# Ternary gate and up weights kept in SBUF, and the first codes and gate product made in the second attention's end

## The chip, the cores and the metric

The kernel runs on one core of one Trainium2 chip. The metric is the device time of one execution in microseconds (us). A core has five engines that run their own instruction streams and meet in semaphores: TensorE (PE, matmuls, with its weight loads shown as PEld), VectorE (DVE), ScalarE (ACT), GpSimd (POOL) and SyncE (SP, which here issues the DMAs). SBUF is the working memory of 128 partitions, PSUM holds the eight banks that TensorE writes.

## The reference, cut to what matters

Four layers of attention and feed-forward run over `x` (2, 256, 512), that is four tiles of 128 rows. The change lies in layer 1: its attention (16 heads with low-rank projections), and its feed-forward, for which the reference computes in this manner:

```python
def int4_quant(x):
    beta = jnp.mean(jnp.abs(x), axis=-1, keepdims=True)
    x_q = jnp.clip(jnp.round(x * SQRT7 / (beta + EPS)), -8, 7)
    return x_q * (beta * SQRT7) / SQRT7
def bitlinear(x, w, scale):
    w_mean = jnp.mean(jnp.abs(w))
    w_q = jnp.clip(jnp.round(w / (w_mean + EPS)), -1.0, 1.0)
    return jnp.einsum('...i,oi->...o', x, w_q * w_mean * scale)
```

The normalised rows are quantised to four bits (the "codes"). Gate and up products with ternary weights (1376 x 512) follow, then relu squared of the gate times the up product, an eight-bit quantisation of that (by its row maximum), and the down product (512 x 1376), which is added to `x`. All three weights must be summed over their absolute values before one of them can be rounded.

## The kernel before, in words

Each layer part is a function with one block, in which every engine has its own program; all engines meet in a barrier between blocks. The order on each engine is written out by hand. Three stages matter: `layer1_attention` (from 73 us to 184 us of the span), `layer1_ffn` (184 to 233 us) and then `layer2_attention`.

**`layer1_attention`** runs 64 steps `u`, one for a head of one of the four row tiles (16 steps a tile, so tile t is done after step 16t + 15). In a step PE makes the scores of step u + 3, turns the exponentials of step u (L976) and mixes; DVE takes the row maximum (`maximum`, L1070); ACT makes the exponentials (L1174) and copies three turned tiles of four out of PSUM (L1183), DVE the fourth (`copy_turned`, L1094). Into these steps DVE has other work woven: at steps 40, 45, 50 and 55 the counts of a bisection that belongs to a later layer (L2394), at steps 53 and 54 the division and addition for the tile before (L1080, L1087), then the row statistics (L1131 to L1137), and at steps 59, 60 and 62 the normalised rows of tiles 0, 1 and 2 (`tile_rows_vector`, L267). These need `rstd`, which POOL makes with one power instruction each (L274). After step 63 the last tile goes through ACT's `copy_mixed` (L1190), PE's `turn_mixed` (L1006), `divide_mixed` and `add_mixed`, and the block ends.

**The ternary weights.** During these steps POOL rounds the weights (`ternary_round_gpsimd`, L400, L402 and L404, three instructions a piece) in 13 pieces: four of gate and four of up (128 x 1376), three of down (128 x 1536) and two small ones of down. SP loads a piece into one of two buffers, and stores the rounded piece to HBM (`ternary_round_sync`, L419). POOL's three `rstd` instructions stand behind all thirteen pieces. The first instructions of `layer1_ffn` on SP read all of it back, six DMAs for gate and up (L1263) and two for down.

**`layer1_ffn`** begins with the statistics of tile 3 on DVE (L257 to L261) while ACT sums the magnitudes of all four tiles (L1288). `quantise4` (L1328) makes the codes of two tiles at a time on DVE: three small instructions, scaling (L1339), rounding (L1342), clipping (L1345), and three small ones for the scales. PE turns the codes (L1422), ACT copies them, and the gate and up products follow in three chunks of columns (512, 512, 352; `gate_up`, L1440). Of each chunk ACT makes relu and square (L1309, L1314), and DVE the product with up (`inner_chunk`, L1363). PE may fill a bank pair again when ACT and DVE have read the chunk two before. For each tile DVE then finds the maximum (`magnitude`, L1368), scales (L1378) and rounds (L1383); PE turns the result (`turn8`, L1435) and makes the down product (`down`, L1464). DVE has two bisection counts ahead of the first chunks (L1390 to L1394). PE's last work in the stage is woven with key and value products for the next layer (`first_group_kv`, L1541), whose weights POOL splits when they are loaded (L1522 to L1531).

## Time and profile before

| what | value |
|---|---|
| median of 3 runs | 852.37 us (851.94 to 855.39) |
| profiled execution, its own time | 853.51 us |
| its span | 851.8 us |
| busy in the span | PE 773.4, PEld 628.2, DVE 692.9, ACT 517.0, POOL 433.0 us |
| mean granted TensorE clock | 0.978 of full speed |
| HBM read and written | 60.28 MB and 5.34 MB |

The span is what the profiler shows from the first to the last instruction; the execution's own time lies 1.7 us above it. PE is busy for 91% of the span, DVE for 81%. Such shares say little of a stage that takes 49 us of 852: in the windows from 184.3 to 233.2 us PE is busy for 38.98 us and DVE for 39.77 us of 48.90, and the granted clock is 0.90. What a change in this stage is worth is read from the timeline there. A timeline row gives start, duration, engine, line and operation, and in brackets how long the engine had been idle before it and what it waited for; a row with xN merges N instructions.

### The profile page before, as it was taken

Reading aid. Unit: us, or ns where it says so; the run is one execution under the profiler, and the core shown is the slowest. Engines: PE = TensorE matmul, PEld = TensorE weight load, DVE = VectorE, ACT = ScalarE, POOL = GpSimd, SP = SyncE. Lnnn points to the kernel's source line nnn. Section 1 sums busy time; section 2 is a strip of 40 time slices with the busy share of each in tenths; the row PEclk is TensorE's granted clock in tenths of the full one; section 3 lists DMA queues with packets and bytes.
Section 4 is the critical chain, followed back from the end, with each engine's and each line's share of the span. In section 5 each row is a group of like instructions: output and inputs, shape, how many; then the busy total and the mean of one; then the engine's idle time right before and its main releaser. Section 6 shows DMA issues by size and latency. Waiting matters only on the chain. (4 is left out here: it accounts for less than half of the span.)

```text
span 851.8 us, 16376 instructions
## 1 busy us (share of the span) xinstructions
PE 773.4 (91%) x5134; PEld 628.2 (74%) x5140; DVE 692.9 (81%) x1766; ACT 517.0 (61%) x1401; POOL 433.0 (51%) x388
## 2 busy tenths in 40 slices
PE   1976799948988999999999999999999999988888
PEld 0474566634677898888888888989888889776447
DVE  7878998969787887887887788788878878876986
ACT  6875789846457657657657656665675675641421
POOL 3236068825134755745746746745754764665110
PEclk9999999978999999999999999999999999999999
DMA  8244136535030320320220320220310210003001
GB/s 308 99 167 157 64 116 218 187 119 181 0 100 1 100 76 1 99 74 0 99 74 0 99 74 0 99 61 13 99 49 25 74 50 25 26 1 118 3 0 50
DMA packets 37773, 66.15 MB, mean 78 GB/s; under 512 B 5537, under 2 KB 17889, under 8 KB 37602
## 3 DMA queue, kind: packets, MB, share of 16 engines
q1 hardware_dynamic: 37730, 65.63, 23.4%
q8 instruction: 21, 0.34, 0.2%
q14 instruction: 22, 0.18, 0.1%
HBM read 60.28 MB, written 5.34 MB: 77 GB/s over the span
## 5 line engine op out<-in xcount | busy, mean ns | idle before, releaser
L2394 DVE TENSOR_SCALAR_CACHE_REDUCE xn<-ctxT,candidate 128x512 bf16<-128x512 f32 x240 | 168.8, 741 | 0.0
L2041 ACT ACTIVATE layer_attention_probs<-xnT,stats 128x512 f32<-128x512 f32 x128 | 93.9, 734 | 114.6 <-DVE stats L2176 114.6
L2188 DVE TENSOR_TENSOR layer_attention_probsT<-bank,layer_attention_probsT 128x512 fp32r<-128x512 f32 x128 | 88.1, 688 | 50.5 <-ACT layer_attention_probsT L2049 49.3
L1780 PE MATMUL bank<-layer_attention_keysT,layer_attention_queriesT 128*128 128x512 f32 x384 | 121.8, 425 | 5.0 <-DVE layer_attention_queriesT L2169 5.0
L1780 PEld LDWEIGHTS bank<-layer_attention_probsT,layer_attention_values 128*128 128x128 f32 x768 | 99.1, 189 | 13.5 <-DVE layer_attention_probsT L2188 5.2
L2049 ACT CAST layer_attention_probsT<-bank 128x512 fp32r<-128x512 f32 x128 | 74.9, 585 | 52.7 <-PE bank L1857 52.6
L1780 PE MATMUL bank<-layer_attention_probsT,layer_attention_values 128*128 128x256 f32 x768 | 102.3, 282 | 4.1 <-DVE layer_attention_probsT L2188 3.0
L1780 PE MATMUL bank<-layer_attention_l_wq,layer_attention_xnT 128*128 128x512 f32 x408 | 99.3, 392 | 0.1
L1780 PEld LDWEIGHTS bank<-layer_attention_l_wkv,layer_context_parts 128*128 128x128 f32 x720 | 88.3, 188 | 2.8
L1780 PE MATMUL bank<-layer_attention_l_wkv,layer_context_parts 128*128 128x256 f32 x720 | 90.3, 278 | 0.0
L1780 PE MATMUL bank<-layer_attention_wo,layer_attention_headsT 128*128 128x512 f32 x336 | 88.8, 406 | 0.0
L2176 DVE CUSTOM_DVE_ANT_0 xnT<-bank,layer_attention_mask 128x512 f32<-128x512 f32 x128 | 87.1, 680 | 0.6 <-PE bank L1780 0.5
L1780 PEld LDWEIGHTS bank<-layer_attention_l_wq,layer_attention_xnT 128*128 128x128 f32 x408 | 75.3, 188 | 16.0 <-issue 0.2
L1723 POOL TENSOR_TENSOR layer_attention_mixed<-layer_attention_mixed,xnT 128x512 f32<-128x512 f32 x30 | 49.0, 1633 | 70.1 <-DMA xnT<-inverse_sums 49.5
L1857 PE MATMUL bank<-ident,layer_attention_probs 128*128 128x128 f32 x512 | 76.9, 273 | 3.0 <-ACT layer_attention_probs L2041 3.0
L1857 PEld LDWEIGHTS bank<-ident,layer_attention_probs 128*128 128x128 f32 x512 | 61.2, 140 | 14.2 <-issue 4.0
L1780 PEld LDWEIGHTS bank<-layer_attention_keysT,layer_attention_queriesT 128*128 128x128 f32 x384 | 63.0, 191 | 11.6 <-issue 5.8
L1780 PEld LDWEIGHTS bank<-layer_attention_wo,layer_attention_headsT 128*128 128x128 f32 x336 | 60.0, 189 | 11.5
L1708 POOL TENSOR_SCALAR layer_attention_ssq<-layer_attention_ssq 128x4 f32<-128x4 f32 x48 | 9.7, 202 | 87.5 <-ACT layer_attention_squares L2000 87.5
L2000 ACT ACTIVATE layer_attention_squares<-bank 128x128 f32<-128x128 f32 x192 | 52.0, 298 | 0.0
L1174 ACT ACTIVATE layer_attention_probs<-bank,layer_attention_negmax 128x512 f32<-128x512 f32 x64 | 44.9, 706 | 11.0 <-DVE layer_attention_negmax L1070 10.7
L1710 POOL TENSOR_TENSOR layer_attention_ssq<-layer_attention_ssq,minus_half 128x4 f32<-128x4 f32 x48 | 48.8, 1018 | 4.0
(340 smaller groups left out, 1645.5 us busy)
## 6 DMA issues: line engine op xcount, KB each, us to landing
layer_attention_l_raw_qo<-in_wqT SPq DMA_DIRECT2D x8, 1024.0 KB, 5.5
layer_attention_l_raw_qo<-in_woT SPq DMA_DIRECT2D x8, 1024.0 KB, 6.6
xnT<-inverse_sums SPq DMA_DIRECT2D x15, 512.0 KB, 3.7
tw_raw<-in_w_gateT SPq DMA_DIRECT2D x8, 688.0 KB, 5.5
tw_raw<-in_w_upT SPq DMA_DIRECT2D x8, 688.0 KB, 4.2
tw_raw<-in_w_downT SPq DMA_DIRECT2D x6, 768.0 KB, 4.6
layer_attention_l_raw_kv<-in_wkvT SPq DMA_DIRECT2D x8, 512.0 KB, 4.8
ternary<-tw_rounded SPq DMA_DIRECT2D x8, 344.0 KB, 2.5
```

The lines of the kernel that those rows point to most:

```text
L1174: a.activation(probs[:, u % 4, :], S[u % 3][:, :], ACT.Exp, bias=negmax[:, tile(u), head(u):head(u) + 1], accum_out=sums[:, tile(u), head( ...
L1708: own(g.tensor_scalar(ssq[:, c, :], ssq[:, c, :], 1.0 / HD, EPS, ALU.mult, ALU.add))
L1710: own(g.tensor_tensor(ssq[:, c, :], ssq[:, c, :], k.minus_half[:, 0:REP], ALU.pow))
L1723: g.tensor_tensor(now, now, factors, ALU.mult).then_inc(S_["mix_scaled"], 1)
L1780: last = pe.matmul(out, stationary[f][a], moving[f][b], start=f == 0 and x == 0, stop=f == count - 1 and x == 2)
L1857: last = pe.transpose(T[u % 2][:, c * P:(c + 1) * P], probs[:, u % 3, c * P:(c + 1) * P], k.ident[:, :])
L2000: return a.activation(squares[:, h, :], source, ACT.Square, accum_out=ssq[:, c, h:h + 1])
L2041: a.activation(probs[:, u % 3, :], masked[:, u % 2, :], ACT.Exp, bias=negmax[:, u:u + 1], scale=-1.0, accum_out=sums[:, u:u + 1]).then_inc ...
L2049: a.copy(probsT[:, 0, p % 2, :, u % 2 * P:(u % 2 + 1) * P], T[u % 2][:, :].rearrange("p (c q) -> p c q", c=CPB)).then_inc(S_["probsT_high" ...
L2176: v.tensor_tensor_reduce(masked[:, u % 2, :], S[u % 2][:, :], mask[:, u % TPB, :], -1.0, 3.4e38, ALU.add, ALU.min, negmax[:, u:u + 1]).the ...
L2188: v.tensor_tensor(probsT[:, 1, p % 2, :, columns], T[u % 2][:, :].rearrange("p (c q) -> p c q", c=CPB), probsT[:, 0, p % 2, :, columns], A ...
L2394: own(k.nc.vector.tensor_scalar((k.flags if flags is None else flags)[:, r % 2], row_tile(k.ctxT, r), k.candidate[:, r:r + 1].bitcast(F32) ...
```

## The change

**Memory.** A new `Region` on the other side of SBUF holds what was allocated apart: the query weights of the attention (`raw_qk`, `wqk`), and over them, once they are spent, the rounded gate and up weights (`gate_up`), then in layer 2 `wo`, `mask` and `mixed`. POOL writes rounded gate and up pieces straight into `gate_up`; only down pieces are still stored to HBM and read back. The pieces come in another order: down first, then gate, then up. From the third gate piece on they overlay `wqk`, so POOL first waits for the last query product (`BESIDE_WQK`).

**`rstd`.** POOL makes it for tile 0 after 6 pieces, for tile 1 after 10, for tile 2 after all 13. DVE makes the rows of tiles 0, 1 and 2 at steps 52, 53 and 61 instead of 59, 60 and 62.

**Codes.** ACT sums the magnitudes of tiles 0 and 1 at steps 57 and 58, and of tile 2 after the last step. DVE scales and rounds the codes of tiles 0 and 1 at step 62, and clips them and makes their scales after step 63. PE turns them ahead of `turn_mixed`, ACT copies them after `copy_mixed`, and as its last work in the block PE waits for all thirteen pieces and makes gate and up of the first chunk of tile 0.

**Feed-forward.** SP issues two DMAs for the down weights and no other ahead of the next layer's. The codes of tiles 2 and 3 are made between the chunks of tiles 0 and 1; the first chunk of tile 1 is taken ahead of the first magnitude. The two bisection counts stand at the end of DVE's program, around the rows for the next layer.

```diff
+def codes_magnitude_scalar(k, n, t, absolute):
+    k.nc.scalar.wait_ge(k.tile_xn, TILES * n + t + 1)
+    if t:
+        k.nc.scalar.wait_ge(k.codes.beta_ready, t)
+    k.nc.scalar.activation(absolute, k.xn[:, t, :], ACT.Abs, accum_out=k.codes.beta[:, t:t + 1])\
+     .then_inc(k.codes.beta_ready, 1)
...
+def codes_rounded_vector(k, h, scaled):
+    v, own, q = k.nc.vector, k.vown, k.codes
+    tiles = range(h * TPB, (h + 1) * TPB)
+    for t in tiles:
+        own(v.tensor_scalar(scaled[t % TPB], k.xn[:, t, :], SQRT7, q.binv[:, t:t + 1], ALU.mult, ALU.mult))
+    own.wait()
+    for t in tiles:
+        own(v.tensor_scalar(scaled[t % TPB], scaled[t % TPB], ROUND, ROUND, ALU.add, ALU.subtract))
+
+
+def codes_clipped_vector(k, h, scaled, codes):
+    k.vown.wait()
+    for t in range(TPB):
+        k.nc.vector.tensor_scalar(codes[t], scaled[t], -8.0, 7.0, ALU.max, ALU.min).then_inc(k.codes.codes_ready, 1)
...
+def gate_up_tensor(k, t, c):
+    pe, q = k.nc.tensor, k.codes
+    c0, c1 = INNER_CHUNKS[c]
+    i = len(INNER_CHUNKS) * t + c
+    for w, bank, ready in ((GATE, k.bank[0:2], q.gate_psum), (UP, k.bank[2:4], q.up_psum)):
+        for f in range(KT):
+            last = pe.matmul(bank[i % 2][:, 0:c1 - c0], k.region.turned[t][:, f, :], k.region.gate_up[:, w, f, c0:c1],
+                             start=f == 0, stop=f == KT - 1)
+        last.then_inc(ready, 1)
...
+        self.raw_qk = view("raw_qk", [HEADS1 * P], F32, 0)
+        self.wqk = view("wqk", [2, HEADS1 * P], F32R, wide)
+        self.gate_up = view("gate_up", [2, KT, INNER], BF16, 0)
+        early = view("turned", [KT, TPB * P], BF16, held)
+        self.turned = [early[:, :, t * P:(t + 1) * P] for t in range(TPB)]
+        self.wo = view("wo", [2, REP2, D], F32R, 0)
+        self.mask = view("mask", [TPB, CTX], F32, 2 * wide)
+        self.mixed = view("mixed", [REP2, SEQ], F32, 2 * wide + 4 * TPB * CTX)
...
+    ROUNDED = (8, 9, 10, 11, 12, 0, 1, 2, 3, 4, 5, 6, 7)
+    BESIDE_WQK = 2
...
+        if w == DOWN:
+            if j >= 2:
+                g.wait_ge(tw.stored[n % 2], 16 * (j // 2))
+            target = tw.rounded[0:rows, n % 2, 0:width]
+        else:
+            if KT * w + f == tw.BESIDE_WQK:
+                g.wait_ge(queries_made, B * HEADS1 // 2)
+            target = k.region.gate_up[:, w, f, :]
+        g.tensor_scalar(target, raw, -ROUND, 1.0, ALU.add, ALU.mult).then_inc(tw.rounded_ready, 1)
...
-                ternary_round_gpsimd(k)
-                for t in range(TILES - 1):
-                    tile_norm_gpsimd(k, following, t)
+                ternary_round_gpsimd(k, 0, 6, S_["queries_psum"])
+                tile_norm_gpsimd(k, following, 0)
+                ternary_round_gpsimd(k, 6, 10, S_["queries_psum"])
+                tile_norm_gpsimd(k, following, 1)
+                ternary_round_gpsimd(k, 10, len(TernaryWeights.PIECES), S_["queries_psum"])
+                tile_norm_gpsimd(k, following, 2)
...
+                for t in range(TPB):
+                    codes_turn_tensor(k, t, early_codes[t], code_bank(t))
                 turn_mixed(TILES - 1)
+                pe.wait_ge(k.codes.turned_ready, 1)
+                pe.wait_ge(k.ternary.rounded_ready, len(TernaryWeights.PIECES))
+                gate_up_tensor(k, 0, 0)
...
-                    if u in (59, 60, 62):
-                        tile_rows_vector(k, following, (59, 60, 62).index(u))
+                    if u in (52, 53, 61):
+                        tile_rows_vector(k, following, (52, 53, 61).index(u))
+                    if u == 62:
+                        codes_inverse_vector(k, 0)
+                        codes_rounded_vector(k, 0, scaled)
...
+                codes_clipped_vector(k, 0, scaled, early_codes)
+                codes_scales_vector(k, 0)
...
+                    if u in (57, 58):
+                        codes_magnitude_scalar(k, following, u - 57, absolute)
+                codes_magnitude_scalar(k, following, 2, absolute)
                 copy_mixed(TILES - 1)
+                for t in range(TPB):
+                    codes_turned_scalar(k, t, code_bank(t))
...
-                quantise4(0)
-                tile_rows_vector(k, n, TILES - 1)
-                quantise4(1)
...
-                bisection_count(k, own, 0, first_flags(k))
-                for c in range(NC):
-                    inner_chunk(0, c)
-                    if c == 0:
-                        bisection_count(k, own, 1, first_flags(k))
+                inner_chunk(0, 0)
+                tile_rows_vector(k, n, TILES - 1)
+                inner_chunk(0, 1)
+                inner_chunk(0, 2)
+                codes_inverse_vector(k, 1)
+                codes_rounded_vector(k, 1, scaled_late)
+                inner_chunk(1, 0)
+                codes_clipped_vector(k, 1, scaled_late, codes_late)
+                codes_scales_vector(k, 1)
...
+                bisection_count(k, own, 0, first_flags(k))
                 for t in range(TPB):
                     tile_rows_vector(k, following, t)
+                bisection_count(k, own, 1, first_flags(k))
```

On VectorE, the steps 51 to 55 of the attention, before (L1070 is the row maximum, L1080 and L1087 the division and addition of a finished tile, L2394 a bisection count):

```order
L1070 TENSOR_REDUCE layer_attention_negmax<-bank 128x1
L1094 COPY layer_attention_probsT<-bank 128x512
L1070 TENSOR_REDUCE layer_attention_negmax<-bank 128x1 x2
L1075 RECIPROCAL layer_attention_inverse<-layer_attention_sums 128x16
L1080 TENSOR_TENSOR layer_attention_mixed<-bank,layer_attention_inverse 128x512
L1070 TENSOR_REDUCE layer_attention_negmax<-bank 128x1
L1087 TENSOR_TENSOR x<-x,layer_attention_mixed 128x512
L1070 TENSOR_REDUCE layer_attention_negmax<-bank 128x1
L1094 COPY layer_attention_probsT<-bank 128x512
L2394 TENSOR_SCALAR xn,counts<-ctxT,candidate 128x512 x2
```

and after (L1195 is the row maximum, L356 the normalised rows):

```order
L1195 TENSOR_REDUCE layer_attention_negmax<-bank 128x1
L1219 COPY layer_attention_probsT<-bank 128x512
L1195 TENSOR_REDUCE layer_attention_negmax<-bank 128x1
L356 TENSOR_SCALAR xn<-x,meanvar,rstd 128x512
L1195 TENSOR_REDUCE layer_attention_negmax<-bank 128x1
L1200 RECIPROCAL layer_attention_inverse<-layer_attention_sums 128x16
L1205 TENSOR_TENSOR layer_attention_mixed<-bank,layer_attention_inverse 128x512
L356 TENSOR_SCALAR xn<-x,meanvar,rstd 128x512
L1195 TENSOR_REDUCE layer_attention_negmax<-bank 128x1
L1212 TENSOR_TENSOR x<-x,layer_attention_mixed 128x512
L1195 TENSOR_REDUCE layer_attention_negmax<-bank 128x1
L1219 COPY layer_attention_probsT<-bank 128x512
L2467 TENSOR_SCALAR xn,counts<-ctxT,candidate 128x512 x2
```

Two row instructions have come in, one ahead of and one behind the division; the third stays near the end.

On ScalarE, the last steps of the attention and the start of the feed-forward, before (L1174 exponentials, L1183 a turned tile, L1190 the mixed tile, L1288 a magnitude):

```order
L1183 COPY layer_attention_probsT<-bank 128x512
L1174 ACTIVATE layer_attention_probs,layer_attention_sums<-bank,layer_attention_negmax 128x512
L1183 COPY layer_attention_probsT<-bank 128x512
L1174 ACTIVATE layer_attention_probs,layer_attention_sums<-bank,layer_attention_negmax 128x512 x2
L1183 COPY layer_attention_probsT<-bank 128x512
L1174 ACTIVATE layer_attention_probs,layer_attention_sums<-bank,layer_attention_negmax 128x512
L1183 COPY layer_attention_probsT<-bank 128x512 x2
L1190 COPY layer_attention_mixedT<-bank 128x512
L923 UNCONDITIONAL_BRANCH
L1279 UNCONDITIONAL_BRANCH
L1288 ACTIVATE layer_ffn_t,layer_ffn_beta<-xn 128x512 x4
L1283 COPY layer_ffn_x4T<-bank 128x4x128 x2
```

and after (L128 is the magnitude, L180 the copy of turned codes):

```order
L1313 COPY layer_attention_probsT<-bank 128x512
L128 ACTIVATE layer_attention_values,codes_beta<-xn 128x512
L1304 ACTIVATE layer_attention_probs,layer_attention_sums<-bank,layer_attention_negmax 128x512
L1313 COPY layer_attention_probsT<-bank 128x512
L128 ACTIVATE layer_attention_values,codes_beta<-xn 128x512
L1304 ACTIVATE layer_attention_probs,layer_attention_sums<-bank,layer_attention_negmax 128x512 x2
L1313 COPY layer_attention_probsT<-bank 128x512
L1304 ACTIVATE layer_attention_probs,layer_attention_sums<-bank,layer_attention_negmax 128x512
L1313 COPY layer_attention_probsT<-bank 128x512 x2
L128 ACTIVATE layer_attention_values,codes_beta<-xn 128x512
L1320 COPY layer_attention_mixedT<-bank 128x512
L180 COPY region_turned<-bank 128x4x128 x2
```

Of the four magnitudes at the stage's head two now stand between exponentials and one ahead of the mixed tile's copy; the copies of the codes follow it ahead of the barrier.

On VectorE, the head of the feed-forward, before:

```order
L1323 UNCONDITIONAL_BRANCH
L257 BN_STATS stats<-x 128x6
L259 BN_AGGR meanvar<-stats 128x2
L261 TENSOR_SCALAR varep<-meanvar 128x1
L1331 TENSOR_SCALAR layer_ffn_beta<-layer_ffn_beta 128x2
L1333 TENSOR_SCALAR layer_ffn_betae<-layer_ffn_beta 128x2
L1335 RECIPROCAL layer_ffn_binv<-layer_ffn_betae 128x2
L1339 TENSOR_SCALAR layer_ffn_t<-xn,layer_ffn_binv 128x512 x2
L1342 TENSOR_SCALAR layer_ffn_t<-layer_ffn_t 128x512 x2
L1345 TENSOR_SCALAR layer_ffn_x<-layer_ffn_t 128x512 x2
```

and after (L1448 is a chunk of gate times up, L147 to L166 the codes of tiles 2 and 3):

```order
L1437 UNCONDITIONAL_BRANCH
L346 BN_STATS stats<-x 128x6
L348 BN_AGGR meanvar<-stats 128x2
L350 TENSOR_SCALAR varep<-meanvar 128x1
L1448 SCALAR_TENSOR_TENSOR layer_ffn_inner<-bank,codes_up_scale,layer_ffn_gate 128x512
L356 TENSOR_SCALAR xn<-x,meanvar,rstd 128x512
L1448 SCALAR_TENSOR_TENSOR layer_ffn_inner<-bank,codes_up_scale,layer_ffn_gate 128x512
L1448 SCALAR_TENSOR_TENSOR layer_ffn_inner<-bank,codes_up_scale,layer_ffn_gate 128x352
L135 TENSOR_SCALAR codes_beta<-codes_beta 128x2
L137 TENSOR_SCALAR codes_betae<-codes_beta 128x2
L139 RECIPROCAL codes_binv<-codes_betae 128x2
L147 TENSOR_SCALAR layer_ffn_t<-xn,codes_binv 128x512 x2
```

The chunks of tile 0 come right behind the statistics, where the codes of tiles 0 and 1 stood.

On TensorE, at the same place, before (L1006 turns the mixed tile, L1422 the codes, L1451 is gate and up):

```order
L1006 MATMUL bank<-ident,layer_attention_mixedT 128x128 x4
L923 UNCONDITIONAL_BRANCH
L1415 UNCONDITIONAL_BRANCH
L1422 MATMUL bank<-ident,layer_ffn_x 128x128 x8
L1451 MATMUL bank<-layer_ffn_wgu,layer_ffn_x4T 128x512 x16
L1451 MATMUL bank<-layer_ffn_wgu,layer_ffn_x4T 128x352 x8
L1422 MATMUL bank<-ident,layer_ffn_x 128x128 x8
L1451 MATMUL bank<-layer_ffn_wgu,layer_ffn_x4T 128x512 x16
```

and after (L189 is gate and up, L173 the turning of codes, L1515 of the eight-bit tile):

```order
L173 MATMUL bank<-ident,layer_attention_values 128x128 x8
L1126 MATMUL bank<-ident,layer_attention_mixedT 128x128 x4
L189 MATMUL bank<-region_gate_up,region_turned 128x512 x8
L1040 UNCONDITIONAL_BRANCH
L1506 UNCONDITIONAL_BRANCH
L189 MATMUL bank<-region_gate_up,region_turned 128x512 x8
L189 MATMUL bank<-region_gate_up,region_turned 128x352 x8
L189 MATMUL bank<-region_gate_up,region_turned 128x512 x16
L189 MATMUL bank<-region_gate_up,region_turned 128x352 x8
L173 MATMUL bank<-ident,layer_ffn_x 128x128 x8
L1515 MATMUL bank<-ident,layer_ffn_x 128x128 x10
```

Eight products stand ahead of the barrier, and the codes of tiles 2 and 3 are turned behind the products of tile 1.

## Rows read from the trace of the kernel before

**Rows 1.** Windows of the trace: stretch, length, busy us (x instructions), PEclk, DMA share.

```profile
165.00:170.00 5.00, 4.77 (x54) 3.13 (x53) 4.96 (x10) 3.61 (x10) 4.72 (x5) 1.00 0.11 34
...
188.50:191.50 3.00, 1.03 (x8) 0.90 (x10) 2.03 (x9) 1.60 (x4) 0.00 (x0) 0.50 1.06 338
...
194.00:196.50 2.50, 2.50 (x7) 0.91 (x6) 2.46 (x8) 0.50 (x2) 0.00 (x0) 0.51 1.11 341
...
210.00:233.20 23.20, 21.66 (x142) 13.43 (x145) 17.09 (x30) 8.96 (x17) 5.63 (x5) 1.00 0.01 1
```

**Rows 2.** Timeline, attention's end: start, us, engine, line, operation, idle before and releaser.

```profile
163.80 0.69 DVE L1070 TENSOR_REDUCE layer_attention_negmax<-bank 128x1 f32<-128x512 f32 x1 [0.30 <-PE bank L968]
...
171.81 0.69 ACT L1174 ACTIVATE layer_attention_probs<-bank,layer_attention_negmax 128x512 f32<-128x512 f32 x1 [2.61 <-DVE layer_attention_negmax L1070]
...
176.54 0.59 ACT L1183 COPY layer_attention_probsT<-bank 128x512 f32<-128x512 f32 x1 [0.94 <-PE bank L976]
...
179.03 0.69 DVE L1094 COPY layer_attention_probsT<-bank 128x512 f32<-128x512 f32 x1 [1.36 <-PE bank L976]
...
180.92 0.58 ACT L1190 COPY layer_attention_mixedT<-bank 128x512 f32<-128x512 f32 x1 [2.15 <-PE bank L992]
...
182.37 0.69 DVE L1080 TENSOR_TENSOR layer_attention_mixed<-bank,layer_attention_inverse 128x512 f32<-128x512 f32 x1 [2.50 <-issue]
```

**Rows 3.** Instructions of lines 1087, 267, 1288: count, minimum/median/maximum in ns, first and last start.

```profile
L1087 DVE TENSOR_TENSOR x<-x,layer_attention_mixed x4: 692/1243/1637, 124.0 to 183.1; 128x512 f32<-128x512 f32 x4
...
L267 DVE TENSOR_SCALAR xn<-x,meanvar,rstd x8: 536/544/550, 175.3 to 240.1; 128x512 f32<-128x512 f32 x8
...
L1288 ACT ACTIVATE layer_ffn_t<-xn x4: 613/622/631, 184.4 to 189.9; 128x512 f32<-128x512 f32 x4
```

**Rows 4.** Timeline, the rounding on POOL.

```profile
111.73 1.49 POOL L400 TENSOR_SCALAR tw_raw<-tw_raw,tw_bound 128x1376 f32<-128x1376 f32 x1 [24.84 <-DVEq L388]
...
163.51 1.62 POOL L400 TENSOR_SCALAR tw_raw<-tw_raw,tw_bound 128x1536 f32<-128x1536 f32 x1 [1.91 <-DMA tw_raw<-in_w_downT]
...
174.69 1.58 POOL L274 TENSOR_TENSOR rstd<-varep,minus_half 128x1 f32<-128x1 f32 x3
```

**Rows 5.** Timeline, feed-forward from its start to the first magnitude, DVE and ACT.

```profile
184.38 0.69 DVE L257 BATCH_NORM_STATS2 stats<-x 128x6 f32<-128x512 f32 x1 [0.59 <-PEq L923]
...
185.73 0.17 DVE L1331 TENSOR_SCALAR layer_ffn_beta<-layer_ffn_beta 128x2 f32<-128x2 f32 x1 [0.24 <-ACT layer_ffn_t L1288]
...
188.05 0.76 DVE L1345 TENSOR_SCALAR layer_ffn_x<-layer_ffn_t 128x512 bf16<-128x512 f32 x2
...
189.32 0.54 DVE L267 TENSOR_SCALAR xn<-x,meanvar,rstd 128x512 f32<-128x512 f32 x1
...
193.14 0.69 ACT L1309 ACTIVATE layer_ffn_relu<-bank,layer_ffn_gate_scale 128x512 f32<-128x512 f32 x1 [1.56 <-PE bank L1451]
...
193.86 0.63 ACT L1314 ACTIVATE layer_ffn_gate<-layer_ffn_relu 128x512 f32<-128x512 f32 x1
...
194.25 0.74 DVE L2394 TENSOR_SCALAR_CACHE_REDUCE xnT<-ctxT,candidate 128x512 bf16<-128x512 f32 x1
...
199.82 1.59 DVE L1368 TENSOR_REDUCE layer_ffn_gamma<-layer_ffn_inner 128x1 f32<-128x1376 f32 x1
...
203.07 0.74 DVE L1363 SCALAR_TENSOR_TENSOR layer_ffn_inner<-bank,layer_ffn_up_scale,layer_ffn_gate 128x512 f32<-128x512 f32 x1
```

**Rows 6.** Timeline, feed-forward, TensorE.

```profile
188.53 1.03 PE L1422 MATMUL bank<-ident,layer_ffn_x 128*128 128x128 bf16 x8 [6.25 <-DVE layer_ffn_x L1345]
...
198.86 3.62 PE L1451 MATMUL bank<-layer_ffn_wgu,layer_ffn_x4T 128*128 128x512 bf16 x16
...
210.87 1.35 PE L1451 MATMUL bank<-layer_ffn_wgu,layer_ffn_x4T 128*128 128x352 bf16 x8 [1.44 <-DVE layer_ffn_inner L1363]
```

**Rows 7.** Timeline, the last of VectorE and of TensorE in the feed-forward.

```profile
229.11 0.55 DVE L267 TENSOR_SCALAR xn<-x,meanvar,rstd 128x512 f32<-128x512 f32 x1 [0.45 <-POOL rstd L274]
...
231.76 1.03 PE L1464 MATMUL bank<-layer_ffn_wd,layer_ffn_x8T 128*128 128x512 bf16 x4
```

228 lines of the change are left out of this document (107 added, 121 removed).

## The prediction

> **What bounds the kernel now.** I read first the windows by engine around the two stages that the change touches, then the timeline of the attention's last steps, then that of the feed-forward. In the attention's last quarter VectorE has no room: between 165 and 170 us it is busy for 4.96 of 5.00 us, and POOL, which rounds weights, for 4.72 [rows 1]. This is where the lead is lost: ScalarE waits 2.61 us for a row maximum at 171.81 [rows 2]. Behind that point nobody is full: ScalarE waits 0.94 us for TensorE at 176.54, VectorE 1.36 us at 179.03 and 2.50 us at 182.37, ScalarE 2.15 us at 180.92 [rows 2]. The feed-forward starts at 184.38. From there to the first magnitude at 199.82 [rows 5] it takes 15.4 us, because codes, turning, copies and the first products follow one another; TensorE waits 6.25 us for the first codes [rows 6], and its granted clock is 0.50 to 0.51 of full speed, the lower level of 1.2 GHz, while it resumes [rows 1]. From 210.87, where the last chunk of tile 2 goes out on TensorE after a wait of 1.44 us for VectorE [rows 6], TensorE is the bound: 21.66 us busy of 23.20 [rows 1], until its last product at 231.76 + 1.03 = 232.79 [rows 7]. VectorE is through at 229.11 + 0.55 = 229.66 [rows 7].
>
> **The attention's end: what is added.** Three things lengthen it.
>
> First, the rows of tiles 0 and 1, 0.54 us each [rows 3], move from behind the full stretch into it. They read and write SBUF while POOL rounds. No row instruction in this trace stands beside the rounding, so its price there is bounded. The addition of line 1087, also between SBUF tensors, takes 0.69 us at its least, its last start being 183.1, when POOL has been through since 174.69 + 1.58 = 176.3 [rows 3, 4]; its median is 1.24 and its longest 1.64, so the neighbour costs 0.55 us in the median. I take 0.54 + 0.55 for each row, 2.2 us, less the 0.30 us that VectorE still waits at 163.80 [rows 2]: 1.9 us. Bounds: 2 x 0.54 - 0.30 = 0.8 below, and 2 x (0.54 + 1.49) - 0.30 = 3.8 above, if each row waits for a whole POOL instruction (1.49, [rows 4]). The place that they leave gives nothing back, since VectorE waits for TensorE there.
>
> The page "SBUF — State Buffer" of the Trainium skill (section "Who interferes with whom") says that VectorE and GpSimd have one pair of ports in common, which an instruction holds to its end, and that a tensor-scalar instruction between SBUF tensors can be of the kind that takes it. By that rule a row would wait for what is left of a POOL instruction, at worst all of it; the trace agrees in kind, 1.64 against 0.69 us for the addition [rows 3], and the rule's worst case is rival (b).
>
> Second, two magnitudes of 0.62 us on ScalarE [rows 3] at steps 57 and 58. The first stands ahead of the exponentials that release the last scores, so it counts whole; the second fits in the 0.94 us that ScalarE waits at 176.54 [rows 2]. 0.6 us, between 0.3 (both but for the 0.94) and 1.2.
>
> Third, behind the turned mixed tile TensorE makes eight products of 512 columns. Sixteen take 3.62 us at full clock [rows 6], so eight take 1.8; beside them run VectorE's division and addition, 0.69 each [rows 2, 3], so some 0.3 us stands out (between nothing and, at the low clock, where six weight loads fit in 2.50 us [rows 1] and eight products take 3.3, 1.9 us).
>
> At nothing I cost the rest. Scaling and rounding of two tiles (188.05 - 185.73 = 2.3 us, [rows 5]) go where the 1.36 us wait was and two rows of 0.54 have left; clipping and scales (189.32 - 188.05 = 1.3 us) fit in the 2.50 us wait; the third magnitude in the 2.15 us wait; the turning of codes beside the copy of the mixed tile (0.58 us, all [rows 2]). If the first cover is gone, up to 2.3 - 1.1 = 1.2 us comes on top; it goes into the range. The stores to HBM that go cost no engine anything here.
>
> Sum: 1.9 + 0.6 + 0.3 = 2.8 us later at the feed-forward's start, between 1.1 and about 8.
>
> **The feed-forward: what is won.** The way to the first magnitude, from the start S: statistics 185.73 - 184.38 - 0.24 = 1.1 us, beside which ScalarE makes relu and square of the first chunk (194.49 - 193.14 = 1.35, [rows 5]). Then the first chunk on VectorE (0.74, [rows 5]) to 2.1, tile 3's row to 2.6, the second chunk when its square is ready (2.8) to 3.5. ScalarE puts tile 3's magnitude (0.62) between, so relu and square of the third chunk end near 4.7, and the chunk itself at 5.4. Codes up to rounding 2.3: 7.7. First chunk of tile 1: 8.4. Clip and scales 1.3: 9.7. POOL splits the next layer's weights from about here, since its loads no longer stand behind six others; I add 0.3 us for that. The first magnitude starts at S + 10.0 instead of S + 15.4, and the chunk that stood behind it at 203.07 is done too (0.7): VectorE is 6.1 us ahead.
>
> TensorE gets less of it. It has nothing between the turning of the codes of tiles 2 and 3 (S + 10.3) and the first rounded tile, which needs at least magnitude and scaling (203.07 - 199.82 = 3.25 us, [rows 5]) plus the rounding: 14.5. It stood idle for 6.25 us at 188.53 and then ran at 0.50 [rows 6, 1]. I expect the low level again. If all of turning and the next sixteen products ran low they would take 16 x 2.50 / 6 = 6.7 instead of 3.6 us and half a microsecond more for turning, less the 1.44 us that TensorE waits for VectorE behind them at 210.87 [rows 6]: 2.2 us lost. If half of them, 1.5 + 0.5 - 1.44 = 0.6. If none, nothing. I take 0.5. So the row of 210.87 comes 6.1 - 0.5 = 5.6 us nearer to S (between 3.9 and 6.6), and from there TensorE's chain is the old one.
>
> The two bisection counts, four instructions of 0.74 at most [rows 5], land behind VectorE's last statistics. VectorE's end moves by -6.1 + 3.0 - 0.45 (its wait for `rstd` at 229.11, now covered, [rows 7]) = -3.6, that is to 226.1, and TensorE's by -5.6 to 227.2, both counted from the old start. TensorE still ends last by 1.1 us. If that cover went, at most some 1 us would show.
>
> **Sum.** +2.8 - 5.6 = -2.8 us. What follows the barrier is unchanged and shifts whole. The profiled execution took 853.5 us, so its like would take 850.7. The median of the runs lies 1.1 us under it at 852.37, which gives 849.6 us.
>
> **Rivals.**
> (a) The attention's end takes the additions nearly free. For it: all the waits of [rows 2] behind 171.81. Against it: the 4.96 of 5.00. Then +0.8 + 0.6 + 0 and -6.3 with TensorE's clock up: -4.9, 847.5 us.
> (b) Each row waits for a whole POOL instruction (3.8), the rounding's cover is half gone (0.6), magnitudes 0.6, product 0.3, against -5.3: 0.0, 852.4 us. For it: the 1.64 us of line 1087. Against it: the median of 1.24.
> (c) Slower: the row of tile 1 at step 53, and all behind it on VectorE, waits for an `rstd` that stands behind ten rounded pieces, and TensorE's new product for all thirteen. Before, thirteen pieces took 174.69 - 111.73 = 63.0 us, 4.8 each in the mean [rows 4]. In that pace ten end near 160, four microseconds ahead of step 53, and thirteen with three `rstd` near 176.5, eight ahead of the product near 185. One piece waited 1.91 us for its load at 163.51 [rows 4]; if every piece did, thirteen would take 63.0 + 13 x 1.9 = 87.7 and end at 199, 14 us after the product's place: +14 - 5.6, about 861 us. It decides from 1 us a piece more: then 13 us more, 189.5 or 4.5 us late. Against it: a gate or up piece waits for no store any more.
> (d) The change does not do what it says: no sign of it, since eight products do stand ahead of the barrier. No chance of its own.
>
> **How the numbers follow.** The forecast has 0.50, (a) 0.25, (b) 0.17, (c) 0.08. A change is told from none here at 0.5%, 4.3 us: faster is below 848.1, slower above 856.6. Below 848.1 lies most of (a) and the lower edge of the forecast, whose own range is 848.0 to 851.3: 0.28. Above 856.6 lies most of (c): 0.07. Within: 0.65. The range for 8 in 10 reaches from (a) past (b), with the attention's upper bounds: 846.9 to 852.8.
>
> **What would show it.** VectorE's row instructions of tiles 0 and 1 near 164 us last 0.54 us or up to 2; ScalarE's long wait behind the bisection update grows from 2.6 by about 2 us; no VectorE wait for POOL at step 53; the feed-forward's statistics start near 187.2; the first magnitude 10 us behind them; TensorE at 0.50 around 202 us; the barrier near 230.4 instead of 233.2. The prediction is wrong if the start lies over 2 us off 187.2, if a wait for POOL shows in the attention, if the stage from its start to the barrier is not 43.3 us (48.9 less 5.6) within 1.2, or if VectorE and not TensorE ends it.

## The result, and the profile after

The changed kernel takes 857.46 us in the median of 22 runs, the kernel before 854.73 of 22 beside it: the medians lie 2.7 us apart. The ratio that is estimated from all runs is 1.0046, with a 95% interval from 1.0034 to 1.0059. That is 3.9 us (2.9 to 5.0) slower, where 849.6 us and a small gain were forecast. The profiled execution took 857.28 us (span 855.4), 3.8 us more than that of the kernel before.

Three places have to be looked at. The first is the attention's end, the timeline of the kernel after (start, length, engine, line, operation, and in brackets the idle time before and its releaser):

```profile
162.92 1.68 DVE L356 TENSOR_SCALAR xn<-x,meanvar,rstd 128x512 f32<-128x512 f32 x1
...
166.00 1.59 DVE L356 TENSOR_SCALAR xn<-x,meanvar,rstd 128x512 f32<-128x512 f32 x1
...
173.54 0.69 ACT L1304 ACTIVATE layer_attention_probs<-bank,layer_attention_negmax 128x512 f32<-128x512 f32 x1 [2.16 <-DVE layer_attention_negmax L1195]
...
180.90 0.69 DVE L1219 COPY layer_attention_probsT<-bank 128x512 f32<-128x512 f32 x1 [0.31 <-PE bank L1096]
...
186.32 0.69 DVE L346 BATCH_NORM_STATS2 stats<-x 128x6 f32<-128x512 f32 x1 [0.66 <-PEq L1040]
```

The rows of tiles 0 and 1 take 1.68 and 1.59 us instead of 0.54. VectorE's wait of 1.36 us at the copy of step 63 [rows 2] is down to 0.31, as it should be. The feed-forward starts at 186.32 instead of 184.38 [rows 5]: 1.94 us late, 2.8 forecast. VectorE does not wait for an `rstd`: rival (c) did not happen.

The second is the feed-forward, in the same view:

```profile
193.55 0.74 DVE L1448 SCALAR_TENSOR_TENSOR layer_ffn_inner<-bank,codes_up_scale,layer_ffn_gate 128x512 f32<-128x512 f32 x1
194.22 1.59 DVE L156 TENSOR_SCALAR layer_ffn_x<-layer_ffn_t 128x512 bf16<-128x512 f32 x2
194.42 1.11 POOL L1596 CAST layer_attention_l_wkv<-layer_attention_l_raw_kv 128x1024 fp32r<-128x1024 f32 x1 [6.37 <-DMA layer_attention_l_raw_kv<-in_wkvT]
...
195.61 2.55 POOL L1599 TENSOR_TENSOR layer_attention_l_wkv<-layer_attention_l_raw_kv,layer_attention_l_wkv 128x512 fp32r<-128x512 f32 x2
...
195.73 1.23 DVE L161 TENSOR_SCALAR codes_betae<-codes_beta 128x2 f32<-128x2 f32 x1
197.00 1.18 DVE L163 TENSOR_SCALAR codes_up_scale<-codes_betae,tw_wscale 128x2 f32<-128x2 f32 x1
198.09 1.92 DVE L164 TENSOR_SCALAR codes_gate_scale<-codes_betae,tw_wscale 128x2 f32<-128x2 f32 x1
198.11 1.88 POOL L1602 CAST layer_attention_l_wq<-layer_attention_l_raw_qo 128x2048 fp32r<-128x2048 f32 x1
200.06 1.58 DVE L1453 TENSOR_REDUCE layer_ffn_gamma<-layer_ffn_inner 128x1 f32<-128x1376 f32 x1
...
203.32 1.82 DVE L1468 TENSOR_SCALAR layer_ffn_x<-layer_ffn_inner 128x1376 bf16<-128x1376 f32 x1
...
205.20 1.36 PE L1515 MATMUL bank<-ident,layer_ffn_x 128*128 128x128 bf16 x11 [8.94 <-DVE layer_ffn_x L1468]
...
231.80 1.89 PE L1538 MATMUL bank<-layer_ffn_wd,layer_ffn_x8T 128*128 128x512 bf16 x7
...
232.50 0.08 DVE L2467 DVE_READ_ACCUMULATOR xnT<-ctxT,candidate 128x1 f32 x1
```

Up to the first chunk of tile 1 all is as forecast or better: it starts 7.2 us behind the stage's start. Then three scale instructions on two elements a partition, 0.16 to 0.23 us each where POOL is quiet, take 1.23, 1.18 and 1.92 us. Each ends where an instruction of POOL's split ends. Clips and scales take 200.06 - 194.22 = 5.8 us instead of 1.3, and the magnitude comes 13.7 us behind the start instead of 10.0. Behind it the rounding takes 1.82 us (0.88 alone), so TensorE waits 8.94 us, longer than the 6.25 of [rows 6]. Its clock falls as forecast (windows of the kernel after: stretch, length, busy us by engine with counts, PEclk, DMA share, GB/s):

```profile
186.30:200.00 13.70, 8.55 (x48) 4.14 (x48) 11.95 (x20) 8.83 (x16) 6.04 (x5) 0.99 0.67 218
200.00:212.80 12.80, 7.38 (x34) 3.98 (x36) 11.00 (x17) 4.44 (x8) 6.20 (x4) 0.61 0.00 0
```

TensorE ends the stage, as forecast (231.80 + 1.89 = 233.7, against 232.6 for VectorE). The next stage starts here, in the kernel before and in the kernel after:

```profile
233.23 0.75 DVE L2293 SCALAR_TENSOR_TENSOR x<-bank,down_scale,x 128x512 f32<-128x512 f32 x1 [3.58 <-PEq L1257]
```

```profile
234.14 0.75 DVE L2366 SCALAR_TENSOR_TENSOR x<-bank,down_scale,x 128x512 f32<-128x512 f32 x1 [1.55 <-PEq L1384]
```

So only 0.9 us of the loss is made where the change is. The rest comes in the third layer, whose instructions are the same in both. Its loop reloads `woT` once a turn, and its products of the `wkv` weights with the context are 624 of one form. The two reload rows, four turns apart, and the products' durations (minimum/median/maximum in ns), before:

```profile
346.04 0.39 SPq L1632 DMA_DIRECT2D layer_attention_l_raw_qo<-in_woT  x1
...
609.42 0.39 SPq L1632 DMA_DIRECT2D layer_attention_l_raw_qo<-in_woT  x1
```

```profile
L1780 PE MATMUL bank<-layer_attention_l_wkv,layer_context_parts x624: 276/276/285, 312.3 to 716.6; 128*128 128x256 f32 x156
```

and after:

```profile
347.98 0.39 SPq L1705 DMA_DIRECT2D layer_attention_l_raw_qo<-in_woT  x1
...
612.64 0.39 SPq L1705 DMA_DIRECT2D layer_attention_l_raw_qo<-in_woT  x1
```

```profile
L1853 PE MATMUL bank<-layer_attention_l_wkv,layer_context_parts x624: 277/281/297, 314.0 to 720.3; 128*128 128x256 f32 x156
```

A turn takes 263.38 / 4 = 65.85 us before and 264.66 / 4 = 66.17 after, every turn alike: 0.32 us a turn, some 2.3 over the seven turns in the trace. The median product of this form takes 5 ns more, and the starts of neighbours lie 119 instead of 114 ns apart; other forms keep their pace.

Single profiles are not exact to a microsecond: a spell at the low clock wanders. In the stretch 260 to 280 us TensorE ran at full clock in the kernel before and at 0.91 in the kernel after:

```profile
260.00:280.00 20.00, 16.55 (x108) 14.32 (x107) 15.03 (x42) 13.73 (x40) 11.83 (x9) 1.00 0.08 24
```

```profile
260.00:280.00 20.00, 16.61 (x93) 14.23 (x91) 13.47 (x39) 13.53 (x39) 11.72 (x10) 0.91 0.04 10
```

The second profile of the kernel before (t0 below) has 0.91 there too, so the change is not its cause; what causes it stays open. Of the twenty profiles only the first of the kernel before has no such spell between 243 and 279 us. Its place shows in the time: from the next stage's first update (233.23 and 234.14 above) to the first reload row shown it takes 114.1 to 115.1 us in the eleven profiles with a spell before 257 us, and 112.8 to 113.8 in the other nine. So two single profiles can differ there by over a microsecond without a cause in the kernel. Below, stage lengths are means over several profiles where there are several.

### The profile page after: what moved, and what is told of

Same layout as the page of the kernel before. It is cut to its first block and busy times, and to the rows that moved or that the text cites. A ratio compares the mean times of both kernels' runs of the same rounds, so it can differ in the third digit from the quotient of the medians.

```text
span 855.4 us, 16356 instructions
## 1 busy us (share of the span) xinstructions
PE 777.2 (91%) x5134; PEld 632.6 (74%) x5140; DVE 696.7 (81%) x1766; ACT 517.7 (61%) x1401; POOL 432.6 (51%) x388
## 5 line engine op out<-in xcount | busy, mean ns | idle before, releaser
L1853 PE MATMUL bank<-layer_attention_l_wkv,layer_context_parts 128*128 128x256 f32 x720 | 93.5, 282 | 0.0
L1853 PEld LDWEIGHTS bank<-layer_attention_l_wkv,layer_context_parts 128*128 128x128 f32 x720 | 91.2, 188 | 2.6
L1853 PE MATMUL bank<-region_wo,layer_attention_headsT 128*128 128x512 f32 x336 | 88.9, 406 | 0.0
L2249 DVE CUSTOM_DVE_ANT_0 xnT<-bank,region_mask 128x512 f32<-128x512 f32 x128 | 87.2, 681 | 0.6 <-PE bank L1853 0.5
L1796 POOL TENSOR_TENSOR region_mixed<-region_mixed,xnT 128x512 f32<-128x512 f32 x30 | 49.2, 1639 | 69.8 <-DVE candidate L2517 49.6
L1853 PEld LDWEIGHTS bank<-region_wo,layer_attention_headsT 128*128 128x128 f32 x336 | 60.0, 189 | 11.6
L363 POOL TENSOR_TENSOR rstd<-varep,minus_half 128x1 f32<-128x1 f32 x24 | 14.7, 617 | 80.3 <-DVE varep L350 40.2
L1304 ACT ACTIVATE layer_attention_probs<-bank,layer_attention_negmax 128x512 f32<-128x512 f32 x64 | 44.8, 706 | 12.5 <-DVE layer_attention_negmax L1195 12.2
```

The costliest lines, as they stand in the source:

```text
L363: g.tensor_tensor(k.rstd[:, t:t + 1], k.varep[:, t:t + 1], k.minus_half[:, 0:1], ALU.pow).then_inc(k.tile_rstd, 1)
L1304: a.activation(probs[:, u % 4, :], S[u % 3][:, :], ACT.Exp, bias=negmax[:, tile(u), head(u):head(u) + 1], accum_out=sums[:, tile(u), head( ...
L1796: g.tensor_tensor(now, now, factors, ALU.mult).then_inc(S_["mix_scaled"], 1)
L1853: last = pe.matmul(out, stationary[f][a], moving[f][b], start=f == 0 and x == 0, stop=f == count - 1 and x == 2)
L2249: v.tensor_tensor_reduce(masked[:, u % 2, :], S[u % 2][:, :], mask[:, u % TPB, :], -1.0, 3.4e38, ALU.add, ALU.min, negmax[:, u:u + 1]).the ...
```

## The experiments

Eighteen runs follow. Ratios are to the kernel before on the same chip, with 95% intervals; s4 and t3 are one execution each and have none. "The stage" is the feed-forward, from its first statistics to the next layer's first update.

**a0: the changed kernel again.**

> The changed kernel once more, unaltered, for the ratio on this chip and for a second profile. Theory A (the excess over the prediction is VectorE waiting for whole POOL instructions, at the rows of tiles 0 and 1 and at clipping and scales of tiles 2 and 3, and is a property of the kernel): ratio 1.003 to 1.006 again, the stage boundaries at 186.3 and 234.1 us within 0.3 us. Theory B (some 1.6 us of the excess is a stretch of TensorE at its lower clock near 275 us in the third layer that comes and goes from execution to execution): the stretch is absent from this profile, or present in that of a kernel that does not have A's waits.

Ratio 1.0051 (1.0031 to 1.0071); the stage 47.5 us, 66.17 us a turn. The attention's boundary lies at 188.1 and not within 0.3 us of 186.3, and the feed-forward's at 235.6 instead of 234.1; 1.0 us of that shift is there before the attention's first row maximum. The loss is a property of the kernel. Theory B fell: the low spell lay in another place and the time was the same.

**e1: POOL's split behind the scales.**

```diff
                 tile_norm_gpsimd(k, n, TILES - 1)
+                g.wait_ge(q.scales_ready, 2)
                 first_group_split(k)
```

> POOL begins the split of the next layer's weights only when VectorE's scales of tiles 2 and 3 are written. Theory A: the three scale instructions of two columns take 0.16 to 0.23 us each again instead of 1.2 to 1.9, the clips 0.76 instead of 1.59; the first magnitude starts at about start + 9.7 instead of + 13.7 us, the stage is 2.5 to 4 us shorter than the 47.8 us, and the ratio falls by 0.003 to 0.0045, to about 1.000. The split then lies beside scaling and rounding of tile 0 and keeps some of the loss there (up to 1 us). Rival (TensorE's low clock behind its idle stretch sets the stage, not VectorE): the stage stays within 1 us of 47.8 although the magnitude comes earlier.

Ratio 1.0005 (0.9991 to 1.0019), against a0's 1.0051, measured beside it. Timeline of e1:

```profile
194.22 0.75 DVE L156 TENSOR_SCALAR layer_ffn_x<-layer_ffn_t 128x512 bf16<-128x512 f32 x2
...
194.89 0.16 DVE L161 TENSOR_SCALAR codes_betae<-codes_beta 128x2 f32<-128x2 f32 x1
195.09 0.23 DVE L163 TENSOR_SCALAR codes_up_scale<-codes_betae,tw_wscale 128x2 f32<-128x2 f32 x1
195.22 0.22 DVE L164 TENSOR_SCALAR codes_gate_scale<-codes_betae,tw_wscale 128x2 f32<-128x2 f32 x1
195.49 1.58 DVE L1454 TENSOR_REDUCE layer_ffn_gamma<-layer_ffn_inner 128x1 f32<-128x1376 f32 x1
195.57 1.04 POOL L1597 CAST layer_attention_l_wkv<-layer_attention_l_raw_kv 128x1024 fp32r<-128x1024 f32 x1 [7.51 <-DVEq L166]
```

The magnitude comes 4.6 us earlier, at start + 9.2, and the stage is 43.0 us, near the prediction's 43.3. One wait, and the failed term is gone.

**e2 and e3: the rows of tiles 0 and 1 later**, alone and with e1's wait.

```diff
-                    if u in (52, 53, 61):
+                    if u in (58, 59, 61):
...
-                    if u in (57, 58):
+                    if u in (59, 60):
```

> The rows of tiles 0 and 1 go from steps 52 and 53 to 58 and 59, where POOL has rounded its last piece, and their magnitudes from steps 57 and 58 to 59 and 60. Theory A: each row takes 0.54 us instead of 1.6 to 1.7, and ScalarE's wait behind the bisection update is shorter by 2 to 3 us, so the feed-forward starts 1.0 to 1.9 us earlier than at 186.3, ratio about 1.003. Rival (the magnitudes, the codes and the product ahead of the barrier make the 1.9 us, not the rows): the start moves by less than 0.5 us.

> Both edits: POOL's split behind the scales and the rows of tiles 0 and 1 at steps 58 and 59. Theory A: the gains add, 1.0 to 1.9 us at the attention's end and 2.5 to 4 us in the feed-forward: about 5 us under the changed kernel, ratio 0.996 to 0.999, some 2 us under the kernel before. Rival (a gain in the first is taken back by a wait in the second, or TensorE ends the stage regardless): less than 3 us under the changed kernel.

e2: 1.0060 (1.0038 to 1.0082), the start at 186.78. e3: 1.0003 (0.9987 to 1.0018), 853.23 us, as e1. Nothing gained, where e3 was expected at 0.996 to 0.999: my theory for the attention's end fell. Timeline of e2:

```profile
169.30 1.45 POOL L511 TENSOR_SCALAR tw_raw<-tw_raw,tw_winv 128x1376 f32<-128x1376 f32 x1
169.49 1.27 DVE L2514 TENSOR_TENSOR found<-found,set_bit 128x8 int32<-128x8 int32 x1
...
170.83 1.34 POOL L521 TENSOR_SCALAR region_gate_up<-tw_raw 128x1376 bf16<-128x1376 f32 x1
170.88 1.31 DVE L2517 TENSOR_TENSOR candidate<-found,bits 128x8 int32<-128x8 int32 x1
...
174.62 0.53 DVE L356 TENSOR_SCALAR xn<-x,meanvar,rstd 128x512 f32<-128x512 f32 x1
```

The rows do take 0.53 us now, but without their delay the bisection's update comes while POOL still rounds, and two of its 128x8 instructions wait instead (0.17 us each in the kernel after, where POOL was through; 0.47 and 0.17 in the kernel before). The loss changes place.

**p1, p2, p3, p4: where SBUF buffers lie.** p1 adds unused bytes to the kernel before; p2, p3 (with e1's wait) and p4 to the changed one.

```diff
 p1         self.ctxT_loaded = self.keep("ctxT_loaded")
+           self.pads = [self.sbuf(f"pad{i}", [P, TILES], F32) for i in range(5)]
 p2, p3     self.codes = Codes(self)
+           self.pad = self.sbuf("pad", [P, TILES], F32)
 p4
+           k.sbuf("pad", [P, TILES], F32, context, side="right")
             k.region = Region(k, context)
```

> The kernel before with 160 bytes per partition of unused SBUF put where the changed kernel has its five small buffers of scales; nothing else differs, not an instruction. The weights of the third layer (wkv2) then begin at an address that is 0 and not 32 modulo 64. Theory P (the third layer is slower in the changed kernel because TensorE's 256-column products of wkv2 with the context start 119 ns apart instead of 114, and that comes from where the left side of SBUF lies): 119 ns here too, the third layer's loop takes 66.17 us a turn instead of 65.84, and the time is 2.0 to 2.6 us above before, ratio 1.0025 to 1.003. Rival (it comes from the context's own place, or from wo, mask and mixed lying in the region, or from the state of the clock in single executions): 114 ns, 65.84 us, ratio 1.000.

> The changed kernel with 32 bytes more on the left side of SBUF, so that wkv2 is again at 32 modulo 64. Theory P: 114 ns, 65.84 us a turn, 2.0 to 2.6 us under the changed kernel, ratio to before 1.002 to 1.003. Rival (the context's place, or the region): 119 ns, the changed kernel's time.

> The same 32 bytes, and POOL's split held until the scales of tiles 2 and 3 are written. Both causes are then gone and what is left is the change itself. Theories A and P together: 1.2 us (its profile-run against before's median in the last measurement, ratio 1.0005) less 2.3 us: ratio 0.997 to 0.999. By the prediction's own sum, +2.8 at the attention's end and -5.6 in the feed-forward, it would be 0.9967.

> The changed kernel with 32 bytes more on the right side of SBUF: the context's parts move from 32 to 0 modulo 64, wkv2 stays at 0. If what counts is that the two operands agree modulo 64: 114 ns and 2.0 to 2.6 us under the changed kernel. If wkv2's own address counts: 119 ns, the changed kernel's time, ratio 1.004 to 1.006.

p1: 1.0021 (1.0001 to 1.0040), 66.1 us a turn. The same instructions as the kernel before, five unused buffers, and its products are those of the kernel after:

```profile
L1781 PE MATMUL bank<-layer_attention_l_wkv,layer_context_parts x624: 277/281/297, 313.2 to 719.2; 128*128 128x256 f32 x156
```

p2: 1.0035 (1.0015 to 1.0056), p3: 0.9985 (0.9964 to 1.0006), p4: 1.0046 (1.0027 to 1.0065); in all three 119 ns and 66.0 us a turn. So placement is the cause, but neither address modulo 64 is the rule. p3's ratio lies where it was expected (0.997 to 0.999), yet not for the expected reason: its products still stand 119 ns apart.

**s1 and s4: more placements.** s1 puts the five small buffers on the right (with e1's wait), so that the left side lies as before; s4 adds 96 bytes on the left.

```diff
 s1
-        small = lambda name: k.sbuf("codes_" + name, [P, TILES], F32)
+        small = lambda name: k.sbuf("codes_" + name, [P, TILES], F32, side="right")
 s4         self.codes = Codes(self)
+           self.pads = [self.sbuf(f"pad{i}", [P, TILES], F32) for i in range(3)]
```

> The changed kernel with POOL's split held until the scales of tiles 2 and 3 are written, and with the five small buffers of scales on the right side of SBUF, so that everything on the left side, wkv2 too, begins where it does in the kernel before (75,936). If wkv2's own address is what counts: 114 ns between its products, 65.8 us a turn, and 851 to 852 us, ratio 0.997 to 0.9985. If it is the context's parts (which now lie 24,736 bytes lower than in the kernel before), 119 ns and the time of the held kernel, ratio 1.000.

> The changed kernel with 96 bytes more on the left side: wkv2 begins at 76,192, which is the address of the kernel before plus 256. If the address modulo 128 or 256 counts: 114 ns between the products of wkv2 and 65.8 us a turn of the third layer's loop. If not (two other shifts by 32 bytes gave 119 ns): 119 ns and 66.0 to 66.2 us.

s1: 1.0021 (1.0001 to 1.0040), 119 ns, 66.2 us a turn, though `wkv2` begins exactly where it did in the kernel before. s4: 114 ns, 65.8 us a turn, 854.56 us in its one execution. What fits all seven is the distance from `wkv2` to the context's parts modulo 128: 64 in the kernel before and s4; 32 in the changed kernel, p1 and s1; 0 in p2 and p4.

**t3: both shifted, the distance kept.** The kernel before with p1's five buffers on the left and three more on the right.

> The kernel before with 160 bytes more on the left, as in the kernel whose products of wkv2 started 119 ns apart, and 96 more on the right: both addresses differ from before (76,096 and 196,480), their difference modulo 128 is 64 again. If the difference decides: 114 ns and 65.8 us a turn. If one of the two addresses alone decides: 119 ns and 66.0 to 66.2 us.

```profile
L1782 PE MATMUL bank<-layer_attention_l_wkv,layer_context_parts x624: 276/276/285, 312.4 to 716.1; 128*128 128x256 f32 x156
```

114 ns and 65.8 us a turn, at two addresses that the kernel before does not use; 853.82 us in its one execution. Against p1 only what lies on the right, the context's parts among it, has moved, by 96 bytes. The distance, and neither address, goes with the pace in all eight placements. The modulus is not settled: worked out from the addresses, the distances of 64, 32 and 0 are 64, 160 and 128 modulo 256, which fits as well.

**t0: the kernel before again.**

> The kernel before, unaltered, as a comparison of a kernel with itself: ratio 1.000 within 0.0015, and a second profile of it. If the third layer's 65.8 us a turn and its 114 ns are properties of the kernel, they are there again; if they were those of one execution, they are not.

1.0006 (0.9989 to 1.0023); 114 ns, 65.8 us a turn. The pace is the kernel's, not one execution's.

**s2: the scales by column.**

```diff
-    own(v.tensor_scalar(q.betae[:, half], q.beta[:, half], SQRT7, 1.0 / SQRT7, ALU.mult, ALU.mult))
+    for o in ones:
+        own(v.tensor_scalar(q.betae[:, o], q.beta[:, o], SQRT7, 1.0 / SQRT7, ALU.mult, ALU.mult))
...
```

> The changed kernel with the three scale instructions of two columns written as six of one column; POOL's split is not held. Theory A in its narrow form (an instruction on two or more elements per partition waits for the end of POOL's instruction, one on a single element does not, as the instructions of one column beside POOL at 201.7 us that took 0.15 to 0.20 us): the six take 0.15 to 0.25 us each, 1.2 us in all instead of 4.3, the first magnitude starts 3 us earlier, the stage is 1 to 3 us shorter. Rival (any instruction between SBUF buffers waits for POOL, whatever its size): the six wait as the three did, the stage keeps its 47.8 us or grows.

Ratio 1.0011 (0.9995 to 1.0026), the stage 45.2 us. Timeline of s2:

```profile
195.97 2.55 POOL L1602 TENSOR_TENSOR layer_attention_l_wkv<-layer_attention_l_raw_kv,layer_attention_l_wkv 128x512 fp32r<-128x512 f32 x2
196.09 0.20 DVE L163 TENSOR_SCALAR codes_betae<-codes_beta 128x1 f32<-128x1 f32 x2
196.33 0.21 DVE L166 TENSOR_SCALAR codes_up_scale<-codes_betae,tw_wscale 128x1 f32<-128x1 f32 x1
...
196.94 1.58 DVE L1456 TENSOR_REDUCE layer_ffn_gamma<-layer_ffn_inner 128x1 f32<-128x1376 f32 x1
```

POOL is at the same work, yet the six end within 0.85 us (196.94 - 196.09). One element a partition does not wait, two do: 0.20 us against 1.18 to 1.92. The Trainium skill, page "VectorE: DVE Perf Modes", section "What auto-detection actually checks", says that a one-source instruction between SBUF tensors takes the mode with both ports if the outermost dimensions that are not one are both even, or equal. By that rule an instruction on two elements takes both ports; the trace agrees, 1.18 to 1.92 us. What it makes of a single element, which has no such dimension, the section does not say; here such instructions did not wait.

**s3: the weights' half alone**, with e1's wait and s1's placement: rows at steps 59, 60 and 62, and the codes, turning and products of tiles 0 and 1 at the feed-forward's head.

```diff
+                codes_inverse_vector(k, 0)
+                codes_rounded_vector(k, 0, scaled4)
+                codes_clipped_vector(k, 0, scaled4, codes4)
+                codes_scales_vector(k, 0)
                 tile_rows_vector(k, n, TILES - 1)
...
-                    for c in range(1 if t == 0 else 0, NC):
+                    for c in range(NC):
```

> Only the half of the change that concerns the weights (rounded into SBUF, no stores and loads of gate and up), with the split held and the small buffers on the right. Rows at steps 59, 60 and 62 as in the kernel before; magnitudes, codes and turning of tiles 0 and 1 and all products stand at the feed-forward's head again. Leaves out nothing of the computation. If the early codes bring what the trace suggests (-5.8 us in the feed-forward against +2.4 at the attention's end): the feed-forward starts 2.4 us earlier than in the held kernel and takes about 48.5 us instead of 43.0, so 3 to 3.5 us above s1_held_codes_right. Rival (the early codes only move work from one stage to the other): within 1 us of it.

1.0122 (1.0100 to 1.0145), 8.5 us above s1, where 3 to 3.5 were expected. The stage takes 51.3 us instead of s1's 43.5, so against s3 the early codes are worth 7.8 us there. The attention is no shorter without them (first row maximum to the stage's start: 99.2 us, against 97.2 in the kernel before): the two 128x8 instructions take 1.20 and 1.31 us here too. What the end costs is then not mainly the codes. This stage is also 2.2 us longer than that of the kernels with the old order (49.1). s3 is no clean half: it keeps the new order for the codes of tiles 2 and 3, which with tile 1's first chunk stand between the chunks and the first magnitude. That comes 17.9 us behind the start, 2.5 later than the 15.4 of the kernel before. So the 7.8 us are not what the early codes are worth against the kernel before.

**t1 and t2: both causes away.** s4's 96 bytes, with POOL's split held to the scales (t2) or until the first inner tile is rounded (t1, `x8_ready` instead of `scales_ready`).

> The changed kernel with 96 bytes more on the left and POOL's split held until the scales of tiles 2 and 3 are written: both causes gone. 65.8 us a turn in the third layer, 42.6 to 43.2 us in the feed-forward, and the time 851 to 852.5 us, ratio 0.997 to 0.9985: the change's own worth, against the prediction's 0.9967.

> The changed kernel with wkv2 and the context's parts 64 bytes apart modulo 128 (96 more bytes on the left), and POOL's split held until the codes of the first inner tile are rounded. Expected over the variant that holds it only to the scales: rounding of tile 0 takes 0.9 us instead of 1.8 and the turning behind it starts about 1 us earlier, so the stage is up to 1 us shorter (42 to 42.6 us) and the time 850 to 851.5 us, ratio 0.996 to 0.998. Rival: the later split meets tile 1's scaling instead, and nothing is gained over the other.

t2: 851.29 us, 0.9974 (0.9956 to 0.9991). t1: 851.44 us, 0.9971 (0.9954 to 0.9988). In t1's profile the rounding takes 0.88 us and TensorE waits 3.3 instead of e1's 4.3 us; the stage is 41.1 us against t2's 43.7, yet the time is the same. In the two profiles 1.4 of the 2.6 us are lost again between the next stage's first update and the first reload row (114.5 against 113.1 us), t1's spell at the low clock lying near 246 us and t2's near 273, and 0.7 in the attention. Whether the medians of twelve are equal for the same reason is open.

**f1 and f2: the short pieces of weights last.** Both on t2; f1 with e2's steps as well.

```diff
-    ROUNDED = (8, 9, 10, 11, 12, 0, 1, 2, 3, 4, 5, 6, 7)
+    ROUNDED = (8, 9, 10, 0, 1, 2, 3, 4, 5, 6, 7, 11, 12)
```

> The corrected kernel (wkv2 and the context's parts 64 bytes apart modulo 128, POOL's split held to the scales), with two more edits: the two 512-column pieces of the down weights are rounded last, as in the kernel before, instead of fourth and fifth, and the rows of tiles 0 and 1 stand at steps 58 and 59. Theory C (the attention's end loses its 2.3 to 2.9 us to long POOL instructions of 1.3 to 1.5 us, at the rows where these stand beside them, and otherwise at two 128x8 instructions of the bisection's update that took 1.20 and 1.31 us): rows 0.54 us each, the update's two instructions 0.5 us at most, the feed-forward starts 1.5 to 2.5 us earlier than with either edit missing, 849 to 850 us, ratio 0.9945 to 0.9965. Rival (the magnitudes, codes and product ahead of the barrier are what the end costs): ratio 0.997 as without the edits.

> The same corrected kernel with only the two short pieces rounded last; the rows of tiles 0 and 1 stay at steps 52 and 53. Theory C: the rows still meet long pieces and may wait 1 us each as in the changed kernel, the update does not wait: between no gain and 2 us over the corrected kernel, by how the rows fall between two POOL instructions; ratio 0.9955 to 0.9975. Rival: ratio 0.997, and the attention's end unchanged whatever the rows do.

f1: 851.48 us, 0.9976 (0.9960 to 0.9992). f2: 850.68 us, 0.9961 (0.9945 to 0.9976). Timeline of f1:

```profile
170.53 0.55 DVE L2520 TENSOR_TENSOR found<-found,set_bit 128x8 int32<-128x8 int32 x1
...
171.20 0.58 DVE L2523 TENSOR_TENSOR candidate<-found,bits 128x8 int32<-128x8 int32 x1
```

The update's waits are down to 0.4 us each, and from step 54 to the feed-forward f1 loses some 0.9 us against the kernel before and t2 some 3.0 (single profiles; t0 lies 0.7 us from the kernel before). Over the whole attention f1 takes 98.3 and f2 98.0 us, where t2 takes 99.1. The mechanism is shown, the gain in time is not: f1 was expected at 0.9945 to 0.9965 and is no faster than t2, and f2's 0.6 us lie within the intervals. f2 is the fastest version by its median, 3.2 us under the kernel before.

f2 and t2 also show what the low clock costs in the feed-forward. TensorE resumes behind the same wait of 4.34 us, 14.3 us behind the start in both, and the products there are the same. Windows from 3.6 us after that, t2 and then f2:

```profile
204.50:206.90 2.40, 2.40 (x7) 0.90 (x6) 2.40 (x3) 0.89 (x2) 2.40 (x2) 0.50 0.00 0
```

```profile
202.60:205.00 2.40, 2.40 (x13) 1.05 (x12) 2.40 (x3) 1.66 (x4) 2.40 (x2) 1.00 0.00 0
```

Seven products against thirteen, at 0.50 and at full clock, and the stage takes 43.7 us in t2 and 42.5 in f2.

## Why the prediction was wrong, point by point

- **The attention's end, +2.8 us.** Size right, cause half right, so the size is in part luck. From the first row maximum to the feed-forward's start the four profiles with the old attention (before, t0, t3, p1) take 96.8 us in the mean (96.3 to 97.2), the eleven with the changed one 99.7 (98.5 to 100.7): +2.9. The rows did wait, 1.68 and 1.59 us, nearer to rival (b)'s price than to mine. But e2, t2 and s3 show that without their wait the bisection's update waits. In t2 the rows stand where they do in the changed kernel and take 0.54 us each, because POOL had idled for 0.40 us: how the instructions fall decides which of them pays. The prediction missed that the long pieces had moved behind the short ones, so that POOL is at instructions of 1.3 to 1.5 us beside the update, where it was at 0.6 to 0.8. With the order put back (f1, f2) the attention takes 98.2 us, still 1.4 above the old one; how that divides among magnitudes, product and the rest no run shows.
- **The way to tile 1's first chunk.** Forecast start + 7.7 us, measured 7.2. Right. The covers held.
- **"Clip and scales 1.3 ... POOL splits the next layer's weights from about here ... I add 0.3 us for that."** This is the step that failed. Clip and scales took 5.8 us, 4.2 more than 1.3 + 0.3. I had POOL's start right (its load landed at 194.4) and had weighed the shared port for rows of 512 elements, but not for instructions on two: I took their wait as small because they are. Each waits until POOL's instruction ends, 1.0 to 1.7 us longer than it takes alone; the two clips wait as well, 1.59 us together instead of 0.75. How they fall counts here too: in p2, p4 and s4 POOL begins 0.4 to 0.5 us behind the first clip instead of 0.2 to 0.3, the clips take 0.75 together, and the magnitude comes 12.2 us behind the start instead of 13.7. With the split held, the mean stage of e1, p3, s1 and t2 is 43.2 us (42.6 to 43.7), the forecast's 43.3. The agreement is closer than the terms: the magnitude came at start + 9.2 and not + 10.0, and the low clock cost more than its 0.5 us (1.2 between t2 and f2 alone).
- **TensorE's low clock, 0.5 us.** The event was right, the size too small where it can be read. Behind one and the same wait of 4.34 us TensorE is back at full clock 17.8 us behind the start in f2 and 20.3 in t2, and the stage is 1.2 us longer in t2. In the changed kernel the wait was 8.94 us, and the part of the clock in its 47.2 us was not measured by itself.
- **Sum of the feed-forward, -5.6 us.** The mean of the four profiles with the old stage is 49.1 us, that of after, a0, s4, p2 and p4 47.2: -1.9. TensorE ended the stage, as forecast.
- **"What follows the barrier is unchanged and shifts whole."** Wrong, and no rival had it. The instructions are unchanged, but the five new small buffers and the region moved `wkv2` and the context's parts relative to each other. p1 prices the move at 1.8 us (0.1 to 3.4), the turns at 2.3; e1 (1.0005) and t2 (0.9974), which differ by the 96 bytes alone but ran on different chips, at 2.6.
- **The sum as measured:** 2.9 - 1.9 + 1.8 = +2.8 us, against 3.9 (2.9 to 5.0). The rest lies within what the intervals leave open. With both unpriced costs away, t2 gains 2.2 us (0.9974, 0.9956 to 0.9991), where the forecast had -2.8: what it did price was about right in sum.
- **The base.** The forecast's 849.6 us started from the median of three runs, 852.37. Of 22 runs it is 854.73, so 2.4 of the 7.9 us between 849.6 and 857.46 are not the change's.
- **Range and chances.** The 0.07 for slower rested on one mechanism, rival (c). Two costs, 4.2 us beyond the 0.3 that was priced and 1.8 us that was put at nothing, were together twice the net gain of 2.8 us that was forecast. The upper edge of 6.6 us for the feed-forward's gain, and with it the 848.0 of the forecast's own range, has no working: VectorE was put 6.1 us ahead.

## What to carry to other kernels

A load that lands earlier starts its consumer earlier: look at what that consumer now stands beside, instruction by instruction, small ones first. Where GpSimd and VectorE work side by side, price a VectorE scaling of two or more elements between SBUF tensors, or an instruction with two SBUF inputs, at anything from nothing to one whole GpSimd instruction, however little it computes, and compare the length of the instructions beside it before and after. A wait that vanishes at one place is a gain only if what stood behind it does not meet the same neighbour. When buffers are added or moved, compare the rates of the hot matmul forms in later, unchanged stages; a few unused bytes can cost as much as the change brings.

## What the runs showed that I had not expected

- A matmul form of 256 columns, float32 in SBUF, starts every 114 or 119 ns by the distance of its two operands modulo 128 bytes: 64 quick, 0 and 32 slow, in eight placements (96 was not tried, and modulo 256 fits as well). Turns of 65.8 against 66.0 to 66.2 us follow.
- A scaling of two elements a partition took up to 1.92 us beside GpSimd, one of one element 0.20 to 0.21.
- A spell at the low clock early in the third layer changes its place from profile to profile, and with it single profiles differ by over a microsecond. Behind one wait of 4.34 us the clock came back at different times, which made one stage 42.5 or 43.7 us long.
